# Attention in a fused block: the last sum and difference of output halves done by an accumulating DMA instead of VectorE, and four product slots instead of two

## The chip, the cores and the metric

The kernel runs on one core of one Trainium2 chip. The metric is the device time of one execution in microseconds (us); less is better. The core's engines are TensorE (PE; PEld are its weight loads), VectorE (DVE), ScalarE (ACT), GpSimd (POOL) and SyncE (SP), which issues DMAs. They run their own instruction lists in order and meet at semaphores.

## The reference

```python
def reference(x, ctx_4096, A_w, B_w, Wq_w, keys):          # x, ctx: (8, 512, 2048)
    # autocorrelation attention, 8 heads of 256 columns
    q, k = _layernorm(x), ctx_4096
    corr = ifft(fft(q, axis=2) * conj(fft(k, axis=2))).real   # along the 512 positions
    w, idx = top_k(corr.transpose(0, 1, 3, 2), 12)            # per batch and channel
    w = softmax(w)
    for i in range(12):
        g = minimum(idx[:, :, None, :, i] + pos, L - 1)       # shifted, held at the last row
        out = out + w[:, :, None, :, i] * take_along_axis(v, g, axis=2)
    x = x + out
    # gated low-rank FFN: 64 experts of rank 8, the 16 best of them per token
    z = _layernorm(x) @ A_w.T * gate
    return x + (z @ B_w.T) * 2.0
```

## The kernel before

The attention is worked off in 32 groups of 512 channels (8 batches, 4 quarters of the columns each). A group has its 512 positions folded into sums and differences of halves, so all transforms along them are small matrix products. The code of an engine is one function `body`, called for i = 0 to 32; step i does the first half of group i (a: spectra of x and of the context, correlation, top 12) and the second half of group i - 1 (b: weights' spectra, products with the context's spectra, transform back, output). The order on each engine is written out by hand, and semaphores tie them. The FFN follows, in 32 tiles of 128 tokens.

The parts of a step that matter here:

- *TensorE* begins with the context's cyclic spectra (`ctx_cyclic`, line 578, four groups into two banks `evac_ps` in turn, so the third waits for ScalarE's copy of the first to `v_cyc`); then spectra of x (591), the negacyclic ones (602, 603), transposes of the weights (636), the first half of the lags (642), the weights' spectra w0 to w3 (528 to 530), the second half of the lags, and the transform back (691, `out_row`). A step is counted here from its first instruction of line 578. That one needs `vf`, the folded context, from POOL (`v_ready`).
- *VectorE* forms products of spectra. For each of six pairs a step (two for x, four for w) it wrote a cosine part and a sine part into a slot of `prod` (lines 928 to 931); there were two slots of four rows. At the end of b it made the output's halves: `att_sb` gets even + odd and even - odd from the banks `pair_ps` (1100, 1101). Behind these come the last stages of the choice (`choose_last`, 999 to 1006).
- *POOL* adds the two parts of a product to `p_f` (x) or `r_f` (w) (1495), and folds the weights (1502 to 1508), x (1473 to 1480) and the context (1485 to 1491).
- *ScalarE* copies the even output rows to `att_sb` (`copy_even`, 1281), at the end of a step behind the weighting of tiles 0 and 1 (1286). Then it begins the next step with the copies to `v_cyc` (1271), exponentials (1306, 1310), two more copies, the minus operations (1275), the weighting of tiles 2 and 3, and the copy to `v_neg`.
- *SP* loads x (379), the context (382), the last row (387) and a group for statistics (391), and stores `att_sb` (435).

The pieces of the VectorE list that end a step, and ScalarE's copy:

```python
if b:
    dve.wait_ge(even_copied, i)
    dve.wait_ge(pair_ready, pair_out(i, 1) + 1)
    nc.vector.tensor_tensor(att_sb[:, 0:2, :], att_sb[:, 2:4, :], pair_ps[:, 2:4, :], ALU.add)
```

Of the kernel before, what the change touches and what calls it, by code (L numbers as in the profile page):

```python
# [135 lines left out]
def build_program(nc, x, ctx, a_w, b_w, wq_w, keys, tables, out):  # L136
# [6 lines left out]
    with ExitStack() as st:  # L143
# [37 lines left out]
        prod = sb("prod", [P, 2, 4, CH])  # L181
# [52 lines left out]
        even_copied, att_done, stored = sem("even_copied"), sem("att_done"), sem("stored")  # L234

# [141 lines left out]
        def _(sp):  # L377
# [30 lines left out]
            def body(k, r, a, b, f, s):  # L408
# [15 lines left out]
                for g in (2,) if is_step(i, 0) else (3, 4) if is_step(i, 1) else (i + 3,):  # L424
                    if g < GPB * (B - 1):
                        sp.wait_ge(stat_used, LT * (g + 1))
                        load_stat(g // GPB - 1, g % GPB, stat_in[:], stat_loaded)
                if is_step(i, GROUPS - 1):
                    last_group(i)
                if is_step(i, GROUPS):  # L430
                    last_step(i)
                    load_others(0, 2, 1)
                if b:
                    sp.wait_ge(att_done, i)
                    sp.dma_start(at_group(att_t, k, r, -1), att_sb[:]).then_inc(stored, 16)

# [46 lines left out]
            def last_step(i):  # L483

                sp.wait_ge(evac_ready, evac_wt(i, 3) + 1)
                for h in range(2):
                    load_rows(0, 2, h)
                load_others(0, 1, 1)
# [320 lines left out]
        def _(dve):  # L809
# [107 lines left out]
            def body(k, r, a, b, f, s):  # L917
# [3 lines left out]
                def products(idx, pair, vs, plus_one):  # L921

                    c_ps, s_ps = (pair_ps[:, 2 * pair + part, :].unsqueeze(1).broadcast_to((P, 2, CH)) for part in range(2))
                    slot = prod[:, pair, :, :]
                    if not (isinstance(idx, int) and idx < 2):
                        dve.wait_ge(add_done, idx - 1)
                    if plus_one:
                        nc.vector.scalar_tensor_tensor(slot[:, 0:2, :], c_ps, 1.0, vs[:, 0:2, :], ALU.add, ALU.mult)
                    else:
                        nc.vector.tensor_tensor(slot[:, 0:2, :], c_ps, vs[:, 0:2, :], ALU.mult)  # L930
                    nc.vector.tensor_tensor(slot[:, 2:4, :], s_ps, vs[:, 1:3, :], ALU.mult).then_inc(prod_ready, 1)  # L931
# [93 lines left out]
                if a:  # L1025
                    for n in range(2):
# [3 lines left out]
                        products(prod_x(i, n), n, v_cyc[cur][:, 3 * n:3 * n + 3, :], False)  # L1030
# [25 lines left out]
                if b:  # L1056
                    for n in range(4):
# [8 lines left out]
                        products(prod_w(i, n), n % 2, vs, blk < 2)  # L1066
# [30 lines left out]
                if b:  # L1097
                    dve.wait_ge(even_copied, i)
                    dve.wait_ge(pair_ready, pair_out(i, 1) + 1)
                    nc.vector.tensor_tensor(att_sb[:, 0:2, :], att_sb[:, 2:4, :], pair_ps[:, 2:4, :], ALU.add)  # L1100
                    nc.vector.tensor_tensor(att_sb[:, 2:4, :], att_sb[:, 2:4, :], pair_ps[:, 2:4, :], ALU.subtract).then_inc(att_done, 1)
# [92 lines left out]
        def _(act):  # L1194
# [69 lines left out]
            def body(k, r, a, b, f, s):  # L1264
# [12 lines left out]
                def copy_even():  # L1277
# [3 lines left out]
                    nc.scalar.activation(att_sb[:, 2:4, :], pair_ps[:, 0:2, :], ACT.Copy).then_inc(even_copied, 1)  # L1281
# [391 lines left out]
```

## Time and profile before

| | |
|---|---|
| median of 3 runs | 2239.98 us (2239.89 to 2240.15) |
| profiled execution, span | 2240.4 us |
| attention, then FFN | the last store of the attention is issued at 1403.62 us |
| TensorE busy | 2170.8 us, 97% of the span |
| VectorE busy | 1712.2 us, 76% |
| POOL busy | 1570.1 us, 70% |
| ScalarE busy | 1222.0 us, 55% |
| DMA | 287.84 MB, 128 GB/s |

The shares are means over two unlike stages; what a change in the attention is worth has to be read from the attention's steps. "Busy" of TensorE holds the modelled ends of its matmuls, which overlap, so small waits do not show in it but in the starts of its instructions.

### The profile page before, as it was taken

How to read it: one execution, taken by the hardware profiler on the slowest of the kernel's cores; microseconds unless marked ns; L12 is line 12 of the kernel's file. 1: busy time of each engine (PE TensorE's matmuls, PEld its weight loads, DVE VectorE, ACT ScalarE, POOL GpSimd, SP SyncE). 2: the span in 40 equal slices, each digit the busy share in tenths (PEclk: the TensorE clock that was granted, in tenths of full speed). 3: DMA queues.
4: the chain of work that ended last, by engine and by line, in shares of the span. 5: the costliest groups of instructions: out<-in, count | busy, mean ns of one | idle time of the engine just before them, and what ended most of it. 6: DMA issues, size and time to landing. Idle time of an engine off the chain costs nothing.

```text
span 2240.4 us, 30428 instructions
## 1 busy us (share of the span) xinstructions
PE 2170.8 (97%) x9664; PEld 1460.5 (65%) x9664; DVE 1712.2 (76%) x4081; ACT 1222.0 (55%) x2486; POOL 1570.1 (70%) x1023
## 2 busy tenths in 40 slices
PE   4899999999999999999999998899999999999999
PEld 2466565565565565565565564687888888787887
DVE  7999999999999999999999999744544444454443
ACT  4576676676676676676655535544434334443431
POOL 6899999999999999999999987433333333333420
PEclk9999999999999999999999999999999999999999
DMA  8132332332332332332321245544444444444431
GB/s 288 65 120 99 111 110 99 116 106 99 118 104 99 118 104 99 118 103 99 103 82 61 91 164 176 186 157 164 151 162 166 167 160 161 157 159 161 164 116 57
DMA packets 110420, 287.84 MB, mean 128 GB/s; under 512 B 7136, under 2 KB 7264, under 8 KB 109152
## 3 DMA queue, kind: packets, MB, share of 16 engines
q1 hardware_dynamic: 110304, 286.45, 37.1%
q8 instruction: 53, 0.87, 0.2%
q14 instruction: 63, 0.52, 0.1%
HBM read 219.32 MB, written 67.11 MB: 128 GB/s over the span
## 4 chain that ended last, share of the span: by engine, by line
PE 77%; DVE 11%; POOL 5%; issue 4%; ACT 2%; DMA 1%; SPq 0%; DVEq 0%; POOLq 0%; ACTq 0%
PE pair L691 7%; PE out L528 5%; PE out L530 5%; PE out L529 5%; PE z L528 5%; PE z L530 5%; PE z L529 5%; PE evac L602 4%; PE evac L603 4%; PE pair L528 4%; PE evac L578 4%; PE pair L530 4%; PE pair L529 4%; PE lag L642 4%; PE pair L591 4%
## 5 line engine op out<-in xcount | busy, mean ns | idle before, releaser
L1549 POOL TENSOR_TENSOR rows<-rows,cin 128x1024 f32<-128x1024 f32 x48 | 117.9, 2456 | 355.8 <-DMA rows<-out_dram 292.8
L691 PE MATMUL pair<-r_f,back 128*128 128x512 f32 x768 | 335.4, 593 | 0.0
L1495 POOL TENSOR_TENSOR r_f<-prod 128x1024 f32<-128x1024 f32 x128 | 306.0, 2402 | 24.0 <-DVE prod L931 22.1
L691 PEld LDWEIGHTS pair<-r_f,back 128*128 128x128 f32 x768 | 143.3, 190 | 167.8 <-issue 167.8
L528 PE MATMUL pair<-w_hi,wts_hi 128*128 128x512 f32 x512 | 206.5, 403 | 4.9 <-DVE w_lo L1049 2.9
L1244 ACT ACTIVATE xt_full<-tp 128x512 f32<-128x512 f32 x128 | 74.8, 584 | 245.4 <-PE tp L547 242.0
L528 PE MATMUL out<-b_hi,zt_hi 128*128 128x512 f32 x512 | 205.8, 402 | 1.5 <-ACT zt_hi L1433 1.5
L528 PE MATMUL z<-a_hi,xt 128*128 128x512 f32 x512 | 203.0, 397 | 1.9 <-DVE xt L888 1.9
L530 PE MATMUL pair<-w_hi,wts_lo 128*128 128x512 f32 x512 | 200.5, 392 | 0.0
L529 PE MATMUL pair<-w_lo,wts_hi 128*128 128x512 f32 x512 | 200.4, 391 | 0.0
L529 PE MATMUL z<-a_lo,xt 128*128 128x512 f32 x512 | 200.1, 391 | 0.0
L530 PE MATMUL z<-a_hi,xt 128*128 128x512 f32 x512 | 200.1, 391 | 0.0
L530 PE MATMUL out<-b_hi,zt_lo 128*128 128x512 f32 x512 | 199.8, 390 | 0.0
L529 PE MATMUL out<-b_lo,zt_hi 128*128 128x512 f32 x512 | 199.3, 389 | 0.0
L1116 DVE COPY scores<-score_sums 128x64 f32<-128x64 f32 x32 | 7.2, 224 | 214.7 <-PE score_sums L751 214.7
L1552 POOL TENSOR_TENSOR rows<-xin,rows 128x1024 f32<-128x1024 f32 x64 | 154.8, 2419 | 9.7 <-DMA xin<-in_x_dram 0.8
L1147 DVE SCALAR_TENSOR_TENSOR rows<-out,rows 128x512 f32<-128x512 f32 x128 | 88.4, 691 | 91.6 <-PE out L530 89.7
L931 DVE TENSOR_TENSOR prod<-pair,v_cyc 128x1024 f32<-128x1024 f32 x128 | 155.6, 1216 | 0.0
L578 PE MATMUL evac<-vf,fwd 128*128 128x512 f32 x248 | 123.8, 626 | 27.6 <-POOL vf L1563 21.0
L1495 POOL TENSOR_TENSOR p_f<-prod 128x1024 f32<-128x1024 f32 x64 | 150.4, 2373 | 0.0
L1502 POOL TENSOR_TENSOR pick<-e 128x254 f32<-128x254 f32 x128 | 93.3, 729 | 61.3 <-ACT e L1286 61.3
L642 PE MATMUL lag<-lags,p_f 128*128 128x128 f32 (+2 forms) x1024 | 132.2, 278 | 3.4 <-DVE e L975 2.8
(193 smaller groups left out, 5619.2 us busy)
## 6 DMA issues: line engine op xcount, KB each, us to landing
out_dram<-att_sb SPq DMA_DIRECT2D x32, 1024.0 KB, 4.3
rows<-out_dram SPq DMA_DIRECT2D x64, 512.0 KB, 3.6
cin<-out_dram SPq DMA_DIRECT2D x64, 512.0 KB, 4.0
xin<-in_x_dram SPq DMA_DIRECT2D x64, 512.0 KB, 3.7
out_dram<-rows SPq DMA_DIRECT2D x64, 512.0 KB, 2.6
vf<-in_ctx_dram SPq DMA_DIRECT2D x31, 1024.0 KB, 5.2
xf<-in_x_dram SPq DMA_DIRECT2D x30, 1024.0 KB, 5.1
stat_in<-in_x_dram SPq DMA_DIRECT2D x28, 1024.0 KB, 5.1
```

The costliest lines, as they stand in the source:

```text
L528: nc.tensor.matmul(out, lhs_hi, rhs_hi, start=start, stop=False)
L529: nc.tensor.matmul(out, lhs_hi, rhs_lo, start=False, stop=False)
L530: return nc.tensor.matmul(out, lhs_lo, rhs_hi, start=False, stop=stop)
L578: nc.tensor.matmul(evac_ps[n % 2][:], fwd[:, n, :], v[:, fold, :], start=True, stop=True).then_inc(evac_ready, 1)
L591: last = nc.tensor.matmul(pair_ps[:, 2 * n + part, :], fwd[:, t, :], xfs[i % 2][:, fold, :], start=True, stop=True)
L642: return nc.tensor.matmul(lag_ps[t % 2][:, cols], p_f[:, row, t * P:(t + 1) * P], lags[:, cols], start=True, stop=True)
L691: return nc.tensor.matmul(pair_ps[:, bank, :], back[:, 3 * bank + n, :], r_f[:, row, :], start=n == 0, stop=n == 2)
L931: nc.vector.tensor_tensor(slot[:, 2:4, :], s_ps, vs[:, 1:3, :], ALU.mult).then_inc(prod_ready, 1)
L1495: nc.gpsimd.tensor_tensor(dst, prod[:, slot, 0:2, :], prod[:, slot, 2:4, :], ALU.add).then_inc(add_done, 1)
L1502: nc.gpsimd.tensor_tensor(sums, up, down, ALU.add).then_inc(folded_of(g, t), 1)
L1549: nc.gpsimd.tensor_tensor(half, first, second, op).then_inc(c_added, 1)
L1552: nc.gpsimd.tensor_tensor(half, xin[:], half, ALU.add).then_inc(x2_added, 1)
```

## The change

The output halves are no longer summed by VectorE. ScalarE copies the even rows into the first half of `att_sb` and, new, the odd rows into slot 2 of `prod` (`copy_odd`). In the next step it copies the even rows once more and the odd rows with the sign turned (`double_halves`), so that `att_sb` is (even, even) and two slots of `prod` are (odd, -odd). POOL issues one DMA of 1 MB that adds the second to the first in SBUF (`sum_halves`), and SP stores `att_sb` in that next step (`store_summed`). Only the very last group is still summed by VectorE. `prod` now has four slots of two rows: VectorE writes the cosine part straight to `p_f` or `r_f` and the sine part to a slot, and POOL adds the slot in place. The waits for the old contents of `p_f`, `r_f` and the slots move from POOL to VectorE; the third and fourth w product wait for the DMA's end.

```diff
@@ -178,7 +178,7 @@
         wts_hi, wts_lo = sb("wts_hi", [P, 16, P], F32R), sb("wts_lo", [P, 16, P], F32R)
-        prod = sb("prod", [P, 2, 4, CH])
+        prod = sb("prod", [P, 4, 2, CH])
         r_f, back = sb("r_f", [P, 8, CH]), sb("back", [P, 12, P])
...
@@ -425,14 +426,19 @@
                         load_stat(g // GPB - 1, g % GPB, stat_in[:], stat_loaded)
+                if i > 1 and not is_step(i, GROUPS):
+                    store_summed(k, r, i - 1)
                 if is_step(i, GROUPS - 1):
...
                 if is_step(i, GROUPS):
-                    last_step(i)
+                    last_step(k, r, i)
                     load_others(0, 2, 1)
-                if b:
                     sp.wait_ge(att_done, i)
                     sp.dma_start(at_group(att_t, k, r, -1), att_sb[:]).then_inc(stored, 16)
+
+            def store_summed(k, r, g):
+                sp.wait_ge(att_summed, 16 * g)
+                sp.dma_start(at_group(att_t, k, r, -2), att_sb[:]).then_inc(stored, 16)
@@ -480,11 +486,12 @@
-            def last_step(i):
+            def last_step(k, r, i):
...
                     load_rows(0, 2, h)
+                store_summed(k, r, i - 1)
                 load_others(0, 1, 1)
@@ -918,17 +925,14 @@
-                def products(idx, pair, vs, plus_one):
+                def products(first, pair, second, vs, plus_one):
...
                     c_ps, s_ps = (pair_ps[:, 2 * pair + part, :].unsqueeze(1).broadcast_to((P, 2, CH)) for part in range(2))
-                    slot = prod[:, pair, :, :]
-                    if not (isinstance(idx, int) and idx < 2):
-                        dve.wait_ge(add_done, idx - 1)
                     if plus_one:
-                        nc.vector.scalar_tensor_tensor(slot[:, 0:2, :], c_ps, 1.0, vs[:, 0:2, :], ALU.add, ALU.mult)
+                        nc.vector.scalar_tensor_tensor(first, c_ps, 1.0, vs[:, 0:2, :], ALU.add, ALU.mult)
                     else:
-                        nc.vector.tensor_tensor(slot[:, 0:2, :], c_ps, vs[:, 0:2, :], ALU.mult)
-                    nc.vector.tensor_tensor(slot[:, 2:4, :], s_ps, vs[:, 1:3, :], ALU.mult).then_inc(prod_ready, 1)
+                        nc.vector.tensor_tensor(first, c_ps, vs[:, 0:2, :], ALU.mult)
+                    nc.vector.tensor_tensor(second, s_ps, vs[:, 1:3, :], ALU.mult).then_inc(prod_ready, 1)
@@ -1027,7 +1031,10 @@
                         dve.wait_ge(minus_done, 4 * i + n + 1)
-                        products(prod_x(i, n), n, v_cyc[cur][:, 3 * n:3 * n + 3, :], False)
+                        if not is_step(i, 0):
+                            dve.wait_ge(lag_ready, CT * i)
+                            dve.wait_ge(add_done, (prod_x(0, n) if is_step(i, 1) else prod_w(i - 1, n)) + 1)
+                        products(p_f[:, 2 * n:2 * n + 2, :], n, prod[:, n, :, :], v_cyc[cur][:, 3 * n:3 * n + 3, :], False)
                         if n == 0 and not (is_step(i, 0) or is_step(i, 1)):
@@ -1063,7 +1070,13 @@
                         vs = (v_cyc if blk < 2 else v_neg)[before][:, 3 * (blk % 2):3 * (blk % 2) + 3, :]
-                        products(prod_w(i, n), n % 2, vs, blk < 2)
+                        if n == 0 and not is_step(i, 1):
+                            dve.wait_ge(pair_ready, pair_out(i - 1, 1) + 1)
+                        if n < 2:
+                            dve.wait_ge(add_done, (prod_x(i, n) if a else prod_w(i - 1, n)) + 1)
+                        elif not is_step(i, 1):
+                            dve.wait_ge(att_summed, 16 * (i - 1))
+                        products(r_f[:, 2 * blk:2 * blk + 2, :], n % 2, prod[:, n, :, :], vs, blk < 2)
                         if n == 0 and s and r == 3:
@@ -1094,11 +1107,11 @@
                     choose_last()
-                if b:
+                if is_step(i, GROUPS):
                     dve.wait_ge(even_copied, i)
                     dve.wait_ge(pair_ready, pair_out(i, 1) + 1)
-                    nc.vector.tensor_tensor(att_sb[:, 0:2, :], att_sb[:, 2:4, :], pair_ps[:, 2:4, :], ALU.add)
-                    nc.vector.tensor_tensor(att_sb[:, 2:4, :], att_sb[:, 2:4, :], pair_ps[:, 2:4, :], ALU.subtract).then_inc(att_done, 1)
+                    nc.vector.tensor_tensor(att_sb[:, 2:4, :], att_sb[:, 0:2, :], pair_ps[:, 2:4, :], ALU.subtract)
+                    nc.vector.tensor_tensor(att_sb[:, 0:2, :], att_sb[:, 0:2, :], pair_ps[:, 2:4, :], ALU.add).then_inc(att_done, 1)
                 if s and r == 2 and k + 2 > 1:
@@ -1278,7 +1291,18 @@
                         act.wait_ge(stored, 16 * (i - 1))
-                    nc.scalar.activation(att_sb[:, 2:4, :], pair_ps[:, 0:2, :], ACT.Copy).then_inc(even_copied, 1)
+                    nc.scalar.activation(att_sb[:, 0:2, :], pair_ps[:, 0:2, :], ACT.Copy).then_inc(even_copied, 1)
+
+                def copy_odd():
+                    act.wait_ge(pair_ready, pair_out(i, 1) + 1)
+                    nc.scalar.activation(prod[:, 2, :, :], pair_ps[:, 2:4, :], ACT.Copy).then_inc(att_done, 1)
+
+                def double_halves(g):
+
+                    act.wait_ge(even_copied, g)
+                    nc.scalar.activation(att_sb[:, 2:4, :], att_sb[:, 0:2, :], ACT.Copy).then_inc(att_doubled, 1)
+                    act.wait_ge(att_done, g)
+                    nc.scalar.activation(prod[:, 3, :, :], prod[:, 2, :, :], ACT.Copy, scale=-1.0).then_inc(att_doubled, 1)
@@ -1328,6 +1352,8 @@
                         minus(v_cyc[cur][:, 3 * n + 2, :], v_cyc[cur][:, 3 * n, :], 6 * i + 2 * n + 1)
+                if i > 1:
+                    double_halves(i - 1)
                 if is_step(i, 1):
@@ -1402,6 +1428,7 @@
                     middle_copy(i, 2)
+                    copy_odd()
                 if is_step(i, GROUPS):
@@ -1409,6 +1436,8 @@
                     copy_even()
+                    if a:
+                        copy_odd()
                 if is_step(i, GROUPS):
@@ -1492,7 +1521,13 @@
                 pool.wait_ge(prod_ready, idx + 1)
-                nc.gpsimd.tensor_tensor(dst, prod[:, slot, 0:2, :], prod[:, slot, 2:4, :], ALU.add).then_inc(add_done, 1)
+                nc.gpsimd.tensor_tensor(dst, dst, prod[:, slot, :, :], ALU.add).then_inc(add_done, 1)
+
+            def sum_halves(g):
+
+                pool.wait_ge(att_doubled, 2 * g)
+                nc.gpsimd.dma_start(att_sb[:], prod[:, 2:4, :, :].rearrange("p n s c -> p (n s) c"),
+                                    accum_op=ALU.add).then_inc(att_summed, 16)
...
@@ -1577,14 +1612,14 @@
                     variance(k + 2)
+                if i > 1:
+                    sum_halves(i - 1)
                 if b:
...
                 if a:
-                    if not is_step(i, 0):
-                        pool.wait_ge(lag_ready, CT * i)
                     for n in range(2):
@@ -1601,11 +1636,9 @@
                 if b:
-                    if not is_step(i, 1):
-                        pool.wait_ge(pair_ready, pair_out(i - 1, 1) + 1)
                     for n in range(4):
                         blk = W_BLOCKS[n]
-                        add_products(prod_w(i, n), n % 2, r_f[:, 2 * blk:2 * blk + 2, :])
+                        add_products(prod_w(i, n), n, r_f[:, 2 * blk:2 * blk + 2, :])
                         if n == 0 and s and r == 3:
```

ScalarE's list from the end of one step into the next, before (`att_sb<-pair` is copy_even, the first `v_cyc<-evac` opens the next step):

```order
L1286 ACTIVATE e<-e,inv_sum 128x512 x2
L1292 ACTIVATE pick<-e 128x4
L1281 ACTIVATE att_sb<-pair 128x1024
L1271 ACTIVATE v_cyc<-evac 128x512 x2
L1306 ACTIVATE e<-e,neg_max 128x512 x2
L1310 ACTIVATE exp_top,exp_sum<-top,neg_max 128x12 x2
L1271 ACTIVATE v_cyc<-evac 128x512 x2
L1275 ACTIVATE v_cyc<-v_cyc 128x512 x2
L1286 ACTIVATE e<-e,inv_sum 128x512 x2
L1292 ACTIVATE pick<-e 128x4
L1271 ACTIVATE v_neg<-evac 128x512
```

and with the change:

```order
L1310 ACTIVATE e<-e,inv_sum 128x512 x2
L1316 ACTIVATE pick<-e 128x4
L1294 ACTIVATE att_sb<-pair 128x1024
L1298 ACTIVATE prod<-pair 128x1024
L1284 ACTIVATE v_cyc<-evac 128x512 x2
L1330 ACTIVATE e<-e,neg_max 128x512 x2
L1334 ACTIVATE exp_top,exp_sum<-top,neg_max 128x12 x2
L1284 ACTIVATE v_cyc<-evac 128x512 x2
L1288 ACTIVATE v_cyc<-v_cyc 128x512 x2
L1303 ACTIVATE att_sb<-att_sb 128x1024
L1305 ACTIVATE prod<-prod 128x1024
L1310 ACTIVATE e<-e,inv_sum 128x512 x2
```

copy_odd (`prod<-pair`) stands ahead of the first v_cyc copies, and the two doubling copies stand between the minus operations and the weighting of tiles 2 and 3.

POOL's list from its fold of x to the additions of products, before:

```order
L1473 TENSOR_TENSOR half_fold<-xf 128x1024
L1474 TENSOR_TENSOR half_fold<-xf 128x1024
L1502 TENSOR_TENSOR pick<-e 128x2x127
L1503 TENSOR_TENSOR pick<-e 128x2x127
L1502 TENSOR_TENSOR pick<-e 128x2x127
L1503 TENSOR_TENSOR pick<-e 128x2x127
L1507 TENSOR_TENSOR pick<-e 128x2
L1508 TENSOR_TENSOR pick<-e 128x2
L1495 TENSOR_TENSOR p_f<-prod 128x1024 x2
L1479 TENSOR_TENSOR xf<-half_fold 128x1024
```

and with the change:

```order
L1502 TENSOR_TENSOR half_fold<-xf 128x1024
L1503 TENSOR_TENSOR half_fold<-xf 128x1024
L1529 DMA att_sb<-prod 128x2048
L1537 TENSOR_TENSOR pick<-e 128x2x127
L1538 TENSOR_TENSOR pick<-e 128x2x127
L1537 TENSOR_TENSOR pick<-e 128x2x127
L1538 TENSOR_TENSOR pick<-e 128x2x127
L1542 TENSOR_TENSOR pick<-e 128x2
L1543 TENSOR_TENSOR pick<-e 128x2
L1524 TENSOR_TENSOR p_f<-p_f,prod 128x1024 x2
L1508 TENSOR_TENSOR xf<-half_fold 128x1024
```

The DMA stands between the fold of x and the folds of the weights of tiles 2 and 3; the additions read their own output.

## Rows read from the trace of the kernel before

**Rows 1.** Stretches table, middle of the attention: us; busy and count per engine, clock, DMA
```profile
440.00:1300.00 860.00, 854.51 (x3143) 509.37 (x3142) 816.99 (x1833) 552.11 (x1244) 810.98 (x580) 1.00 0.30 101
```

**Rows 2.** The same table, two successive steps
```profile
727.54:769.07 41.53, 41.51 (x153) 24.65 (x152) 39.66 (x90) 27.40 (x64) 39.06 (x27) 1.00 0.32 108
...
769.07:811.71 42.64, 41.61 (x154) 24.65 (x153) 39.89 (x93) 30.76 (x70) 40.66 (x36) 1.00 0.31 105
```

**Rows 3.** Timeline, TensorE: start, us, line, what, count, idle before
```profile
686.01 3.93 PE L578 MATMUL evac<-vf,fwd 128*128 128x512 f32 x8
...
695.79 1.02 PE L603 MATMUL evac<-vf,fwd 128*128 128x512 f32 x2
...
696.79 1.12 PE L602 MATMUL evac<-vf,fwd 128*128 128x512 f32 x2
...
727.54 2.64 PE L578 MATMUL evac<-vf,fwd 128*128 128x512 f32 x5
```

**Rows 4.** Timeline of the same step, POOL
```profile
695.43 0.73 POOL L1502 TENSOR_TENSOR pick<-e 128x254 f32<-128x254 f32 x1 [1.77 <-ACT e L1286]
...
698.48 4.70 POOL L1495 TENSOR_TENSOR p_f<-prod 128x1024 f32<-128x1024 f32 x2
...
708.04 2.41 POOL L1485 TENSOR_TENSOR half_fold<-vf 128x1024 f32<-128x1024 f32 x1
...
715.36 2.36 POOL L1495 TENSOR_TENSOR r_f<-prod 128x1024 f32<-128x1024 f32 x1 [0.17 <-DVE prod L931]
...
718.04 2.36 POOL L1495 TENSOR_TENSOR r_f<-prod 128x1024 f32<-128x1024 f32 x1 [0.33 <-DVE prod L931]
...
725.13 2.36 POOL L1491 TENSOR_TENSOR vf<-half_fold 128x1024 f32<-128x1024 f32 x1
```

**Rows 5.** Timeline of the same step, VectorE
```profile
690.05 1.21 DVE L1100 TENSOR_TENSOR att_sb<-att_sb,pair 128x1024 f32<-128x1024 f32 x1
...
704.40 0.88 DVE L961 TENSOR_TENSOR lag<-e,lag 128x254 f32<-128x254 f32 x2 [0.32 <-ACT e L1297]
...
716.75 1.22 DVE L931 TENSOR_TENSOR prod<-pair,v_cyc 128x1024 f32<-128x1024 f32 x1
```

**Rows 6.** Timeline of the same step, TensorE's weight loads
```profile
687.96 0.30 PEld L578 LDWEIGHTS evac<-vf,fwd 128*128 128x128 f32 x2 [0.79 <-ACT v_cyc L1271]
...
696.79 0.30 PEld L602 LDWEIGHTS evac<-vf,fwd 128*128 128x128 f32 x2 [0.81 <-ACT v_neg L1271]
...
703.23 0.97 PEld L642 LDWEIGHTS lag<-lags,p_f 128*128 128x128 f32 x8 [0.21 <-POOL p_f L1495]
```

**Rows 7.** Timeline of the same step, ScalarE
```profile
686.41 1.01 ACT L1281 ACTIVATE att_sb<-pair 128x1024 f32<-128x1024 f32 x1
...
687.32 1.31 ACT L1271 ACTIVATE v_cyc<-evac 128x512 f32<-128x512 f32 x2
...
691.43 1.15 ACT L1275 ACTIVATE v_cyc<-v_cyc 128x512 f32<-128x512 f32 x2
...
694.63 1.38 ACT L1286 ACTIVATE e<-e,inv_sum 128x512 f32<-128x512 f32 x2 [2.05 <-DVE inv_sum L1004]
...
696.16 0.58 ACT L1271 ACTIVATE v_neg<-evac 128x512 f32<-128x512 f32 x1
```

**Rows 8.** Timeline of the same step, SP's issues
```profile
700.52 0.37 SPq L382 DMA_DIRECT2D vf<-in_ctx_dram  x1
```

**Rows 9.** DMA issues of that step: KB each, us to landing
```profile
vf<-in_ctx_dram SPq DMA_DIRECT2D x1, 1024.0 KB, 5.2
```

**Rows 10.** End of the attention: timelines of ScalarE, POOL, SP; TensorE's waits
```profile
1361.35 0.21 ACT L1292 ACTIVATE pick<-e 128x4 f32<-128x4 f32 x1
...
1360.74 0.73 POOL L1502 TENSOR_TENSOR pick<-e 128x254 f32<-128x254 f32 x1 [4.36 <-ACT e L1286]
...
1318.97 1.51 SPq L443 DMA_DIRECT2D rows<-out_dram  x2
...
PE pair L612 <- DVE att_sb L1101: 5.3, 1, 5.3
```

More of the change, by code:

```diff
@@ L234, in build_program @@
         even_copied, att_done, stored = sem("even_copied"), sem("att_done"), sem("stored")
+        att_doubled, att_summed = sem("att_doubled"), sem("att_summed")
         rows_loaded = [[sem(f"rows_loaded{n}_{h}") for h in range(2)] for n in range(RING)]
@@ L1557, in _ @@
             pool.wait_ge(v_loaded, 16)
-            first = prod[:, 1, :, :]
+            first = prod[:, 2:4, :, :].rearrange("p n s c -> p (n s) c")
             nc.gpsimd.tensor_tensor(first[:, 0:2, :], vf[:, 0:4:2, :], vf[:, 1:4:2, :], ALU.add)
```

## The prediction

> **What bounds the kernel now.** I read a table by stretch, then single steps of the attention, then one of them on each engine. In the middle of the attention TensorE is busy 854.5 of 860 us at a granted clock of 1.00, VectorE 95% and POOL 94% [rows 1]. Three engines are nearly full, so the question is which waits end last. A step lasts 41.53 us; every fourth, which computes normalizers, lasts 42.64 [rows 2].
>
> Take the step that starts at 686.01. The next one starts at 727.54, and POOL finishes its vf at 725.13 + 2.36 = 727.49, which TensorE's first group needs; TensorE has by then just ended its output products [rows 3, 4]. So POOL and TensorE arrive together. POOL's part of that tie begins at VectorE's fourth w product, which ends at 716.75 + 1.22 = 717.97 [rows 5]: POOL adds it at 718.04 and makes three passes over vf behind it without a pause. That product itself waits for TensorE's spectrum. Behind it the work of both is fixed, so a step becomes longer or shorter by what TensorE loses ahead of it.
>
> It loses little there. The third matmul group of a step needs the bank that ScalarE copies to v_cyc: its weights are loaded at 687.96 behind that copy, which starts at 687.32 [rows 6, 7]. The negacyclic group at 696.79 waits for ScalarE's v_neg, which ends at 696.16 + 0.58 = 696.74. In other groups of this kind the next starts 0.86 us behind the last (two matmuls of 0.43); here it is 1.00 from 695.79, and the pair takes 0.10 longer [rows 3]. That is 0.25 us. POOL has the last place: the lag matmuls at 703.23 wait for the second p_f addition, which ends at 698.48 + 4.70 = 703.18 [rows 4, 6]. For VectorE's output sums TensorE waits once only, in the last step.
>
> **The change part by part.**
>
> *Removed from VectorE:* two operations of 1.21 us a step, 2.3 us as they overlap by a tenth [rows 5]. VectorE then stands earlier at its pick of tiles 2 and 3. But the next v_neg on its list needs the spectrum that TensorE ends shortly before 696.79, and at the lag sums (704.40) it waits for ScalarE's copy of TensorE's lags already [rows 5]. Nothing of the 2.3 us passes that point, so I cost it at no gain; what could gain is priced under the rivals.
>
> *Added to ScalarE at the border of steps:* copy_odd has the form of copy_even and stands between it and the first copy to v_cyc. copy_even starts at 686.41, the next instruction at 687.32 [rows 7]. So copy_odd costs 0.91 us at the place for which TensorE's third group waits, in every step. ScalarE gets there no sooner, since what is ahead of copy_even hangs on VectorE's lag sums of tiles 2 and 3, in an unbroken list from the fourth w product.
>
> *Added to ScalarE behind its minus operations:* two copies of 128x1024, at 0.91 each by the same row, and 0.1 for the end of the last. The minus pair ends at 691.43 + 1.15 = 692.58 [rows 7], or at 693.49 when it is 0.91 later; the doubled halves are there at 695.41. The weighting of tiles 2 and 3, now at 694.63 after 2.05 us of waiting for VectorE [rows 7], starts at about 695.3, since VectorE's picks come early enough. So the removed work pays for two thirds of the added. ScalarE's v_neg ends 0.66 us later, at 697.4; TensorE, itself 0.91 later, wants it at 697.56. Here it may win back up to 0.25, which leaves 0.66 of the 0.91.
>
> *Added to POOL:* sum_halves waits for both copies and issues a DMA ahead of the folds of tiles 2 and 3. POOL waits 1.77 us just there, until 695.43 [rows 4]. Behind it stand the folds, both p_f additions (TensorE waits for the second without any slack), the x folds, the first vf pass and all w additions. With an issue of d us the folds start at 695.41 + d, and because of ScalarE's weighting not before 696.1: a shift by the larger of 0.65 and d. No POOL instruction of this trace issues a DMA. From below I take SP's issue of 1 MB, 0.37 us [rows 8]; from above a POOL pass over 128x1024, 2.36 us [rows 4]. I take d = 1.0, near the 0.73 us of POOL's short operation [rows 4], because an issue handles 128 rows and not their elements.
>
> The Trainium skill, "DMA: Bandwidth & Descriptors", section "SWDGE vs HWDGE vs iDMA", speaks against this change: a DMA issued by GpSimd has its descriptors computed in software on GpSimd's own cores. Its Specifications give about 1 us to the first byte against 0.6 for SP. No row here shows either; an estimate by that page makes the shift 1.0 us, and the sum the same.
>
> So a step grows by max(0.66, 0.65, d) = 1.0 us; these lie in one another and are not added. In steps with normalizers POOL is the later of the two by 1.11 us [rows 2] and its shift counts in full, 1.0 again. From the lag matmuls on all engines move by the same amount, and POOL's w additions keep their waits of 0.17 and 0.33 us [rows 4].
>
> *The transfer:* 1 MB, read twice (both sides of the sum) and written once. The plain load of 1 MB lands in 5.2 us [rows 9]; I take 10, and 5.2 to 15.6 as bounds. VectorE's third w product waits for it. That product ends just ahead of 715.36 [rows 4] after two operations of 1.22, so starts at 712.9, or 713.9 in the longer step, 17.5 us behind the issue at 696.4: hidden. The store then has until copy_even of the same step (686.41 + 41.53 = 727.94), hidden too, and stands on SP behind the x and vf loads. The vf load is issued at 700.52 [rows 8] and lands 5.2 later; POOL needs it at 708.04 [rows 4]: 2.3 us of cover against a transfer that may still run.
>
> *In-place additions, four slots:* the additions keep their size: no cost. The waits for the old rows and slots move to VectorE and are over long before. The third w product no longer waits for POOL's slot, but the fourth waits for TensorE: no gain.
>
> *The end of the attention:* in step 32 TensorE waits 5.3 us for VectorE's sums, until 1362.8. copy_odd stands there behind ScalarE's middle copy, 1361.35 + 0.21 [rows 10], and ends at about 1362.5: the same. But now the doubling follows (until 1364.4), then the issue (1365.4), and only then the folds of tiles 2 and 3, which begin at 1360.74 today [rows 10]. TensorE's last transposes wait for these: 4.6 us. SP's first loads for the FFN stage (1318.97, [rows 10]) now stand behind a store that waits for a transfer, some 13 us later; POOL's first row sum is late by it, and the w additions and outputs of step 31, by an estimated 3 us. TensorE's 5.3 us wait takes that up. I add 5 for the end.
>
> **Sum.** 30 steps (2 to 31) x 1.0 = 30, plus 5 = 35. The FFN stage has none of this. The profiled execution has 2240.4 us, 0.4 over the median of 2239.98; with the median, 2275. Bounds: d = 0.37 gives 30 x 0.66 + 4 = 24, or 2264; d = 2.36 gives 71 + 6, or 2317.
>
> **The rivals.**
>
> *The issue on POOL is dearer (0.16).* At d of 2 us and more the same sum gives 30 x d + 6: 2306 at 2.0, 2317 at 2.36. For it: nothing here bounds a software issue. Against: POOL's short operation has 0.73 us in all [rows 4].
>
> *The transfer is slow or in the way (0.12).* If it lands more than 17.5 us after its issue, VectorE's third w product waits, the fourth and POOL's vf passes behind it, and each us counts 30 times: at 19.5 us 60 more, 2335. If it still runs when vf is loaded, the two share the queues: a vf load 3 us later is still covered (2.3 and the step's own 1.0), one 4.5 us later costs 0.7 after POOL's two small waits: 2296. For it: three passes at the loads' rate are 15.6. Against: the DMA share of a step is 0.32 [rows 2].
>
> The Trainium skill, "Collectives: The Full Stack", section "The bandwidth ceiling: the fold count and why AG ≠ RS ≠ AR", says of an adding transfer that its second source read makes it slow and not the arithmetic. No row here shows one; by that rule it lands in time.
>
> *Faster (0.06).* If VectorE's 2.3 us reached ScalarE ahead of the border, copy_odd would be free, the wait at 696.79 (0.25) would go, and steps would shorten by 0.25: 2240 - 8 + 4, or 2236. That with an end that costs nothing is 2232. The point from which it decides is 0.9 us of such lead at copy_even, with d under 0.7 as well. For it: VectorE is 95% busy. Against: the chain ahead of the border starts at a product that waits for TensorE.
>
> *No change that can be told (0.04).* A tenth of a us a step, if ScalarE's 0.91 were covered and POOL's issue fell into its 1.77 us.
>
> **How the numbers follow.** My forecast (d up to 1.8) has 0.62; its own range is 2258 to 2300. The rivals to the slower side have 0.28, of which about two thirds lie up to 2318, which takes in the upper bound of d. Below 2258 lie the 0.10 of the other two. So the range is 2258 to 2318, with some 0.2 outside. A measurement of this kernel tells about 0.2% from no change, 4.5 us; slower by more: 0.62 + 0.16 + 0.12 = 0.90, faster 0.06, the same 0.04.
>
> **What the profile will show.** Right: the weight load of the third group waits some 0.9 us longer for ScalarE's v_cyc; steps of 42.2 to 42.6 us; VectorE idle before its first v_neg and longer before the lag sums; an issue on POOL and its folds 0.7 to 1.3 us later in the step; the lag matmuls waiting for p_f. Wrong: steps at 41.5 or under (ScalarE's copy is covered), waits of VectorE for the DMA's semaphore, waits of POOL for vf from DMA, a store that keeps copy_even. The prediction fails most easily by d, of which no row speaks.

## The result, and the profile after

The changed kernel takes 2265.8 us (median of 4 runs, 2264.6 to 2267.2) against 2240.1 for the kernel before on the same chip: a ratio of 1.011, interval 1.0096 to 1.0125. The forecast was 2275 within 2258 to 2318, and "slower". The span grew from 2240.4 to 2264.2 us, by 23.8. Of these, 29 steps (2 to 30) of 42.44 us in place of 41.86 make 0.58 x 29 = 16.8, and the part from the start of step 31 to the end makes 6.8 (935.1 for 928.3). None of it is in the FFN: from the last output product of step 32 to the end it is 846.2 us for 846.8. Steps of the changed kernel vary more. Two successive ones, by stretch (columns as in [rows 1]), the first with a TensorE that starts late because it waited for vf, the second with a punctual one:

```profile
693.92:735.47 41.55, 41.16 (x153) 24.75 (x153) 36.74 (x84) 29.15 (x65) 39.92 (x28) 1.00 0.46 134
735.47:777.70 42.23, 41.17 (x154) 24.75 (x153) 37.50 (x88) 29.80 (x67) 39.90 (x28) 1.00 0.45 131
```

VectorE is busy 36.7 to 37.5 us of a step, 2 to 3 us less than in the ordinary step of [rows 2], and nothing came of it. DMA share is 0.46 for 0.32. TensorE's granted clock is 1.00 as before. The waits of the changed kernel from 440 to 1300 us (us in total, times, longest) say where the time went:

```profile
DVE v_neg L944 <- PE evac L610: 51.9, 21, 2.6
PEld evac L585 <- ACT v_cyc L1284: 32.5, 41, 2.1
POOL att_sb L1529 <- ACT prod L1305: 22.2, 20, 1.8
POOL half_fold L1514 <- DMA vf<-in_ctx_dram: 15.1, 20, 1.8
PE evac L585 <- ACT v_cyc L1284: 10.2, 15, 1.2
PE evac L585 <- POOL vf L1520: 7.6, 10, 1.1
PE lag L649 <- POOL p_f L1524: 5.6, 20, 0.5
```

VectorE's 2.3 us have become a wait for TensorE's spectrum, 2.5 us a step. TensorE waits at three places: for v_cyc at the third context group, for POOL's p_f at the lag matmuls, for POOL's vf at the start of a step (this one it had before, 4.3 us in 5 steps). POOL waits for the load of vf from DMA, and no such wait stands in the kernel before. In 9 of the steps it is 0.8 to 1.8 us long, in the others some 0.2 us.

ScalarE at the border of the step that starts at 693.92 (timeline, to be compared with [rows 7]):

```profile
693.52 1.01 ACT L1294 ACTIVATE att_sb<-pair 128x1024 f32<-128x1024 f32 x1
694.43 1.02 ACT L1298 ACTIVATE prod<-pair 128x1024 f32<-128x1024 f32 x1
695.33 1.21 ACT L1284 ACTIVATE v_cyc<-evac 128x512 f32<-128x512 f32 x2
...
700.23 1.05 ACT L1303 ACTIVATE att_sb<-att_sb 128x1024 f32<-128x1024 f32 x1
701.18 1.05 ACT L1305 ACTIVATE prod<-prod 128x1024 f32<-128x1024 f32 x1
702.13 1.33 ACT L1310 ACTIVATE e<-e,inv_sum 128x512 f32<-128x512 f32 x2
```

copy_odd costs 0.90 us from start to start (694.43 to 695.33; 0.91 was costed), the doublings 0.95 each, and the weighting starts without a wait. POOL in the same step (to be compared with [rows 4]):

```profile
702.53 0.90 POOL L1529 DMA_DIRECT2D att_sb<-prod  x1 [0.95 <-ACT prod L1305]
703.15 1.04 POOL L1537 TENSOR_TENSOR pick<-e 128x254 f32<-128x254 f32 x1
703.84 1.03 POOL L1538 TENSOR_TENSOR pick<-e 128x254 f32<-128x254 f32 x1
...
706.22 4.95 POOL L1524 TENSOR_TENSOR p_f<-p_f,prod 128x1024 f32<-128x1024 f32 x2
710.89 2.61 POOL L1508 TENSOR_TENSOR xf<-half_fold 128x1024 f32<-128x1024 f32 x1
713.23 2.63 POOL L1509 TENSOR_TENSOR xf<-half_fold 128x1024 f32<-128x1024 f32 x1
716.08 2.42 POOL L1514 TENSOR_TENSOR half_fold<-vf 128x1024 f32<-128x1024 f32 x1 [0.22 <-DMA vf<-in_ctx_dram]
```

The issue has a row of 0.90 us, but the next instruction starts 0.62 behind it. Then something the forecast had no term for: each POOL instruction behind the issue ends some 0.3 us later than it used to (folds 1.04 for 0.73, the p_f pair 4.95 for 4.70), while they still start 0.68 apart. Whoever waits for an end is later by that. The transfers of the stretch 440 to 1300 (KB each, median us from issue to landing):

```profile
att_sb<-prod POOLq DMA_DIRECT2D x21, 1024.0 KB, 8.6
xf<-in_x_dram SPq DMA_DIRECT2D x20, 1024.0 KB, 10.1
vf<-in_ctx_dram SPq DMA_DIRECT2D x20, 1024.0 KB, 7.9
```

The adding DMA lands in 8.6 us, within the bounds of 5.2 to 15.6. The load of x, issued 0.6 us behind it, takes 10.1 us for 5.1, and the vf load behind that 7.9 for 5.2 [rows 9].

### The profile page after: what moved, and what is told of

It is laid out like the page before. It is cut to its first block, busy times and chain, and to the rows that moved or that the text cites. A ratio compares the mean times of both kernels' runs of the same rounds, so it can differ in the third digit from the quotient of the medians.

```text
span 2264.2 us, 30395 instructions
## 1 busy us (share of the span) xinstructions
PE 2167.8 (96%) x9664; PEld 1467.3 (65%) x9664; DVE 1645.7 (73%) x4019; ACT 1297.4 (57%) x2579; POOL 1596.0 (70%) x1054
## 4 chain that ended last, share of the span: by engine, by line
PE 55%; POOL 14%; ACT 11%; DVE 11%; issue 6%; DMA 3%; SPq 0%; DVEq 0%; ACTq 0%; POOLq 0%
PE out L535 5%; PE out L537 5%; PE out L536 5%; PE z L535 5%; PE z L537 5%; PE z L536 5%; POOL p_f L1524 5%; PE pair L535 4%; PE pair L537 4%; PE pair L536 4%; PE tp L554 3%; POOL r_f L1524 2%; ACT v_cyc L1284 2%; DMA vf<-in_ctx_dram 2%; PE score_sums L567 2%
## 5 line engine op out<-in xcount | busy, mean ns | idle before, releaser
L1524 POOL TENSOR_TENSOR r_f<-r_f,prod 128x1024 f32<-128x1024 f32 x128 | 304.5, 2401 | 15.1 <-DVE prod L935 14.8
L1524 POOL TENSOR_TENSOR p_f<-p_f,prod 128x1024 f32<-128x1024 f32 x64 | 158.3, 2624 | 0.0
L649 PEld LDWEIGHTS lag<-lags,p_f 128*128 128x128 f32 x1024 | 124.4, 192 | 19.2 <-POOL p_f L1524 13.2
## 6 DMA issues: line engine op xcount, KB each, us to landing
xf<-in_x_dram SPq DMA_DIRECT2D x30, 1024.0 KB, 10.1
```

The lines of the kernel that those rows point to most:

```text
L649: return nc.tensor.matmul(lag_ps[t % 2][:, cols], p_f[:, row, t * P:(t + 1) * P], lags[:, cols], start=True, stop=True)
L1524: nc.gpsimd.tensor_tensor(dst, dst, prod[:, slot, :, :], ALU.add).then_inc(add_done, 1)
```

## The experiments

Eleven kernels were run. "Before" was measured again with each of the three groups: 2241.3, 2240.4 or 2240.8 us, so times of different groups compare to about 1 us. Each edit is told against the changed kernel unless it says otherwise. Six of the kernels leave out the sum and difference of the halves, or do it for a part only. Where the DMA is gone, the store and VectorE's third product wait for the last thing that is left instead (copy or doubling).

**Slots alone.** The kernel before, with nothing but the four slots, the in-place additions and their waits.

```diff
-        prod = sb("prod", [P, 2, 4, CH])
+        prod = sb("prod", [P, 4, 2, CH])
...
-                nc.gpsimd.tensor_tensor(dst, prod[:, slot, 0:2, :], prod[:, slot, 2:4, :], ALU.add).then_inc(add_done, 1)
+                nc.gpsimd.tensor_tensor(dst, dst, prod[:, slot, :, :], ALU.add).then_inc(add_done, 1)
```

> The kernel before with the four slots alone: VectorE writes the cosine part straight to p_f or r_f, POOL adds in place, and the waits for old rows are VectorE's; output sums, store and ScalarE are as before. Theory (the loss comes from copies at ScalarE's border of steps and from POOL's DMA issue): this part costs and gains nothing, 2240, within 2 us. Rival (the layout costs, by waits moved to VectorE or by additions that read their own output): 2245 or more. Rival (the slots are a gain that the rest eats): 2235 or less.

Measured: 2234.2 us, ratio 0.997 (0.9958 to 0.9981). My theory of no gain was wrong: this part is a gain of 7 us, and this kernel beats both. VectorE's waits before, in the stretch 440 to 1300, had one line that is gone with four slots:

```profile
DVE prod L928 <- POOL r_f L1495: 14.7, 17, 1.3
```

The step with normalizers and the one behind it became shorter together by 0.9 us (42.6 and 41.5 became 42.4 and 40.8), and step 1 by 1.7; the others stayed.

**Two slots.** The kernel of the last experiment, with slot `n % 2` and the old wait.

```diff
-                        products(r_f[:, 2 * blk:2 * blk + 2, :], n % 2, prod[:, n, :, :], vs, blk < 2)
+                        dve.wait_ge(add_done, prod_w(i, n) - 1)
+                        products(r_f[:, 2 * blk:2 * blk + 2, :], n % 2, prod[:, n % 2, :, :], vs, blk < 2)
```

> The kernel before with GpSimd's additions in place and VectorE holding the waits on lag_ready and pair_ready, but with two product slots and the old wait for each (a product waits for the addition two before it). With four slots it was 2234.2 against 2241.3. The kernel before has VectorE waiting for GpSimd's r_f additions 14.7 us over 20 steps, the four-slot kernel none. If the slots are the gain, two slots give 2239 to 2242; if the gain is that GpSimd no longer waits in its queue for the lag and output products, it stays at 2233 to 2236.

Measured: 2241.7, ratio 1.0004 (0.9995 to 1.0014). The gain is that of the slots; adding in place and moving the waits give none.

**copy_odd alone.** No doubling copies and no DMA. With it goes VectorE's sum, as in the change.

```diff
-                if i > 1:
-                    double_halves(i - 1)
...
-                if i > 1:
-                    sum_halves(i - 1)
```

> The changed kernel without the DMA and without the two doubling copies: copy_odd alone is left of ScalarE's added work; the sum and difference are left out, so the stored halves hold the even rows and an old value. With both doublings but no DMA it was 2240.6, with the old VectorE sum and the four slots 2234.2. If copy_odd makes the 6 us between these (0.91 us before the v_cyc copies, less what VectorE's free time gives), it stays at 2239 to 2242. If the doubling copies make it (the weighting and so GpSimd's folds 1.9 us later), it is at 2233 to 2236; my step on the copies said that two thirds of them are covered, so I expect 2237 to 2240, nearer the first.

Measured: 2241.1, ratio 0.9999 (0.9989 to 1.0008): 7 us above the four slots, as the first of the two answers had it.

**Doublings too, no DMA.** As the last, with double_halves kept.

```diff
-                if i > 1:
-                    sum_halves(i - 1)
```

> The changed kernel without the accumulating DMA: all three copies of ScalarE stay, the store waits for the two doubling copies, and the sum and difference are left out, so the output holds even rows alone. Theory (ScalarE's 0.9 us at the border in the steps that do not start late is part of the loss, POOL's issue the other): 2252 to 2260. Rival (transfer and its issue are all of it): 2242 or less. Rival (ScalarE is all of it): 2264 or more.

Measured: 2240.6, ratio 0.9996 (0.9986 to 1.0005). My theory of 2252 to 2260 was wrong and the first rival right: the two doubling copies cost nothing as they stand here, and with the DMA come 25 us.

**The same bytes by SyncE.** A plain copy in place of the adding DMA.

```diff
+                if i > 1:
+                    sp.wait_ge(att_doubled, 2 * (i - 1))
+                    sp.dma_start(att_sb[:], prod[:, 2:4, :, :].rearrange("p n s c -> p (n s) c")).then_inc(att_summed, 16)
```

> The changed kernel with the 1 MB from prod to att_sb as a plain copy issued by SyncE at the same point of the step (behind both doubling copies), instead of the adding DMA issued by GpSimd; the addition itself is left out, so the stored halves hold only the odd rows. No transfer at all gave 2240.6, the change 2265.8. If the cost is GpSimd's issue (0.62 us of its queue and the slower folds and first additions behind it, over 30 steps), this kernel is at 2238 to 2244. If the cost is the traffic beside the other loads (they land 2.5 to 5 us later in the changed kernel), it is at 2252 to 2266. Between the two: both have a share.

Measured: 2242.0, ratio 1.0006 (0.9996 to 1.0015). The copy lands in 8.8 us, as long as the adding one, but it stands 0.4 us behind the load of x on the same queue. The loads beside it land in 6.7 (x) and 6.8 (vf). Nearly all of it is hidden: POOL waits for vf in five steps, 2.7 us in all. The traffic costs some 1.4 us when SyncE issues it, which is no more than the intervals leave open.

**A GpSimd instruction in place of the DMA.**

```diff
-                nc.gpsimd.dma_start(att_sb[:], prod[:, 2:4, :, :].rearrange("p n s c -> p (n s) c"),
-                                    accum_op=ALU.add).then_inc(att_summed, 16)
+                nc.gpsimd.tensor_tensor(pad[:], pad_in[:], pad_in[:], ALU.add).then_inc(att_summed, 16)
```

> The changed kernel with a GpSimd addition of 128 x 216 (by the folds' 0.73 us for 128 x 254, about 0.62 us) on a buffer of its own in the place of the DMA, with the same wait for both doubling copies; the sum and difference are left out. If the price is the time of GpSimd's queue alone (0.62 us, after a wait for ScalarE that comes before the folds' own), it reaches most of the change's 2265.8: 2256 to 2266. If this time hides in the 1.7 us that GpSimd waits for the weighting anyway, it is at 2240 to 2246, and the cost is what the DMA does to the instructions behind it (folds 1.04 for 0.73, additions 2.64 for 2.37).

Measured: 2245.0, ratio 1.0016 (1.0007 to 1.0026). Its steps are those of the kernel without the DMA, 41.81 us on average in both, so 0.5 us of queue hides in POOL's wait for the weighting: the folds start 9.53 us into a step in this kernel and 9.54 without (steps 8 to 27). What it costs stands at the end, 933.1 for 928.3 us from step 31 on. There POOL's last folds wait behind the doubling of step 31's halves. Timeline of this kernel:

```profile
1363.49 0.54 POOL L1530 TENSOR_TENSOR pad<-pad_in 128x216 f32<-128x216 f32 x1 [8.14 <-ACT prod L1306]
1363.99 0.72 POOL L1537 TENSOR_TENSOR pick<-e 128x254 f32<-128x254 f32 x1
```

and without the DMA, where the same fold waits for the weighting only:

```profile
1359.52 0.72 POOL L1532 TENSOR_TENSOR pick<-e 128x254 f32<-128x254 f32 x1 [4.37 <-ACT e L1310]
```

**A plain copy by GpSimd.** The 1 MB, without the addition.

```diff
-                nc.gpsimd.dma_start(att_sb[:], prod[:, 2:4, :, :].rearrange("p n s c -> p (n s) c"),
-                                    accum_op=ALU.add).then_inc(att_summed, 16)
+                nc.gpsimd.dma_start(att_sb[:], prod[:, 2:4, :, :].rearrange("p n s c -> p (n s) c")).then_inc(att_summed, 16)
```

> The changed kernel with GpSimd's DMA as a plain copy of the same 1 MB, issued at the same place, without the addition: the sum and difference are left out. The same bytes by a plain copy on SyncE's queue gave 2242.0, the adding DMA from GpSimd 2265.8. If the issue by GpSimd makes the 24 us, this stays at 2262 to 2267; if the addition does (a longer or a harder transfer), it is at 2242 to 2246.

Measured: 2250.3, ratio 1.0038 (1.0023 to 1.0052), between the two answers. The end is that of the last kernel (932.6 us), and a step is 0.18 us longer. The padding instruction was a little too small a stand-in: the DMA starts 9.14 us into a step where the padding started at 8.99, it holds the queue for 0.60 us where that held it for 0.54, and so the folds start at 9.74 for 9.53, past what POOL's wait can hide. Groups of POOL instructions, 440 to 1300 us (busy, mean ns | idle before):

```profile
L1529 POOL DMA_DIRECT2D att_sb<-prod x21 | 12.1, 575 | 25.5 <-ACT prod L1305 25.5
L1524 POOL TENSOR_TENSOR p_f<-p_f,prod 128x1024 f32<-128x1024 f32 x42 | 98.6, 2363 | 0.0
```

**An eighth of the adding DMA.** The first 16 partitions only.

```diff
-                nc.gpsimd.dma_start(att_sb[:], prod[:, 2:4, :, :].rearrange("p n s c -> p (n s) c"),
+                nc.gpsimd.dma_start(att_sb[0:16, :, :], prod[0:16, 2:4, :, :].rearrange("p n s c -> p (n s) c"),
```

> The changed kernel with the adding DMA cut to the first 16 of the 128 partitions (an eighth of the bytes and, if each row of a partition is a packet, of the packets); the other partitions' sum and difference are left out. If the cost is that of starting a DMA on GpSimd whatever its size (0.62 us of the queue, 0.9 us of the row), it stays at 2258 to 2266 and the row stays near 0.9 us. If GpSimd's time goes with the number of pieces (4,464 packets in all), the row shortens to 0.3 to 0.6 us, the folds behind it are no longer stretched, and the time is 2242 to 2250.

Measured: 2255.6, ratio 1.0063 (1.0046 to 1.0079), between the two answers and in neither. The same groups of this kernel:

```profile
L1529 POOL DMA_DIRECT2D att_sb<-prod x21 | 16.8, 802 | 26.1 <-ACT prod L1305 26.1
L1524 POOL TENSOR_TENSOR p_f<-p_f,prod 128x1024 f32<-128x1024 f32 x42 | 103.1, 2586 | 0.0
```

With a plain copy of 1 MB the additions behind it keep their 2.36 us; with an adding one of 128 KB they have 2.59. The later ends come with the adding kind of DMA, not with the bytes (an eighth of them gives most of the effect), and not with GpSimd's issuing as such.

**The issue behind both p_f additions.**

```diff
-                if i > 1:
-                    sum_halves(i - 1)
...
                         add_products(prod_x(i, n), n, p_f[:, 2 * n:2 * n + 2, :])
+                if i > 1:
+                    sum_halves(i - 1)
```

> The changed kernel with POOL's accumulating DMA issued behind both p_f additions instead of ahead of the folds of tiles 2 and 3. Theory: the lag matmuls no longer wait for p_f, the third group still waits for v_cyc; the issue now stands ahead of the w additions: 2256 to 2264. Rival (traffic): the transfer now lies in the middle of the vf load, POOL waits for vf: 2268 or more.

Measured: 2256.9, ratio 1.007 (1.0053 to 1.0087), as the theory had it: 9 us of the 25 are back. Folds and p_f are as before (0.73 and 2.37), the vf load lands undisturbed (5.2 us); now the two x folds take 2.67. Steps 2 to 30 give back 11 us, and the part from step 31 on is 3.8 us longer still (938.9 for 935.1).

**Issue and doublings later.** The last edit, and the doublings moved to where ScalarE waits for its second v_neg.

```diff
-                if i > 1:
+                if i > 1 and not a:
                     double_halves(i - 1)
...
                     minus(v_neg[cur][:, 2, :], v_neg[cur][:, 0, :], 6 * i + 5)
+                    if i > 1:
+                        double_halves(i - 1)
```

> The changed kernel with both doubling copies moved behind the weighting, the first v_neg copy and its minus, where ScalarE waits 1.5 us for TensorE anyway, and GpSimd's DMA issued behind both first additions (alone that gave 2256.9). If the late weighting, and so late folds, is what is left of the cost, the steps fall by the 1.9 us less the 1.7 us that GpSimd idled for it, and the time is 2240 to 2250; if the traffic of the transfer is what is left, it stays at 2252 to 2258, and it could lose where the transfer (8.6 us from 705) lands behind the third product's slot (free at 716).

Measured: 2254.6, ratio 1.0059 (1.0042 to 1.0076), where 2240 to 2250 was hoped for. The earlier folds bring 2 us at most; POOL then waits for VectorE's product instead (27.0 us in 21 steps), and in 7 steps VectorE's product waits for the transfer (9.1 us), which is no longer hidden there.

**copy_odd behind the next step's first v_cyc copies.**

```diff
                         evac_from(part, evac_cyc(i, part), v_cyc[cur][:, part, :])
+                    if i > 1:
+                        copy_odd(i - 1)
...
                     copy_even()
-                    if a:
-                        copy_odd()
```

> The changed kernel with copy_odd moved behind the first two copies to v_cyc of the next step. Theory: the wait of 0.9 us that TensorE's third group has for v_cyc in every other step goes, but POOL's shift (about 0.9 us at the folds) stays and now shows alone, at the lag matmuls and at vf: 2250 to 2260. Rival (the transfer's traffic or POOL alone set the growth): no change, 2264 to 2268. If the copy's place is all of it: 2245 or less.

Measured: 2293.3, ratio 1.0233 (1.0216 to 1.025), a loss of 27 us where all three answers had a gain or no change. The third group no longer waits (the x spectra start 3.70 us into a step), but copy_odd now stands ahead of the third v_cyc copy, the minus operations, the doublings and the weighting, which starts at 9.10 us for 8.56. So the negacyclic groups wait for v_cyc, 1.1 us a step (L609 below). The transfer now starts 0.1 us ahead of the load of x and lands in 12.1 us, and the wait for vf nearly doubles. How the 27 us divide between these was not tested. Its waits, 440 to 1300 us:

```profile
POOL half_fold L1514 <- DMA vf<-in_ctx_dram: 28.3, 20, 2.6
PEld evac L609 <- ACT v_cyc L1284: 22.0, 20, 1.1
PE lag L649 <- POOL p_f L1524: 12.8, 20, 0.7
PE evac L585 <- POOL vf L1520: 12.5, 17, 1.1
```

## Where a step's time goes

From the trace of each kernel I took, for steps 8 to 27, how long after the step's first matmul TensorE starts its x spectra, its lag matmuls, its w products and its output products, and averaged each over the 20 steps:

| kernel | x spectra | lags | w products | outputs | step |
|---|---|---|---|---|---|
| before | 3.79 | 16.21 | 18.19 | 31.20 | 41.80 |
| slots alone | 3.78 | 16.12 | 18.03 | 31.03 | 41.55 |
| copy_odd alone | 4.60 | 16.64 | 18.35 | 31.35 | 41.81 |
| doublings too, no DMA | 4.55 | 16.60 | 18.31 | 31.30 | 41.81 |
| plain copy by GpSimd | 4.54 | 16.59 | 18.46 | 31.47 | 41.99 |
| an eighth of the adding DMA | 4.55 | 16.60 | 18.66 | 31.66 | 42.17 |
| the change | 4.31 | 16.36 | 18.60 | 31.71 | 42.51 |
| issue behind p_f | 4.28 | 16.33 | 18.08 | 31.15 | 42.04 |

Read along a row against the row above. copy_odd puts 0.82 us ahead of the x spectra (4.60 for 3.78) and loses more than half of it again: 0.52 is left at the lags, 0.32 at the w products, 0.26 in the step. A TensorE that is 0.8 us late no longer waits for v_neg nor for p_f. GpSimd's plain DMA adds 0.16 between lags and w products (1.87 for 1.71), the wait for p_f. The adding one makes that 2.06 even with an eighth of the bytes, 0.19 more: the p_f additions start when they did (12.77 and 12.79 us into the step), and the second one ends 0.20 later. The whole transfer adds 0.29 behind the outputs (10.80 for 10.51 to the end of the step): POOL's pass over vf began late, since vf landed late. The next step's TensorE then starts late and finds v_cyc ready, which is why its x spectra stand at 4.31 and not 4.55, and why steps vary.

## Why the prediction was right, point by point

- **VectorE's 2.3 us bring nothing:** right; they are the 51.9 us of waits for TensorE's spectrum.
- **copy_odd 0.91 at the third group, 0.66 kept:** the delay is right (0.82 on average, 0.90 in ScalarE's rows), what is kept was sized too high. I took back 0.25 at v_neg, and the table has 0.30 by the lags. But I let the rest stand, and another 0.26 is won back there and behind. Of 0.66, 0.26 was left.
- **Doublings two thirds covered, ScalarE later by 0.65:** their cost is nothing in the time (2240.6 for 2241.1), and they are covered nearly whole. I carried the 0.91 undiminished down ScalarE's list. Averaged over steps 8 to 27, the minus pair ends only 0.42 later than in the four-slot kernel, the weighting starts 0.22 later and the first v_neg copy 0.17 (0.91, 0.65 and 0.66 were costed).
- **The issue on POOL, d = 1.0:** the queue was held for 0.62 us, near the lower bound of 0.37. That ScalarE's shift and POOL's lie in one another held up to what POOL's wait can hide: a hold of 0.54 us cost a step nothing more, one of 0.60 that starts 0.15 us later added 0.18, of which 0.16 is the p_f wait. The step that failed in size is the one that let a step grow by d, 1.0. A step grew by 0.58, which is 0.82 above the four-slot kernel less 0.24 that the slots gave. It came from terms of which I had two, both too large: copy_odd and the queue. The ends that come 0.2 to 0.3 us late I had not, and the wait for vf only as a rival. That the total came out near the forecast is in part luck, since the terms that were too large stood in for those that were missing.
- **The transfer is hidden:** right for VectorE's third product and the store. Wrong for the vf load. I gave it 2.3 us of cover and named its delay as a rival; it lands 2.7 us later, and POOL waits 0.75 us a step for it (15.1 over 20), one of the signs that I had named for being wrong. This rival took place in small, 0.29 to 0.34 a step.
- **In-place additions and slots at nothing:** wrong, 7 us of gain. I looked at one ordinary step, where the fourth product waits for TensorE, and not at the step with normalizers, where VectorE waits for a slot up to 1.3 us. Waits of 0.7 us for a slot stand in ordinary steps too, and the length of these did not change without them.
- **The end, 5 us:** 6.8, with the growth of step 31 in it, which the forecast counted among its 30 steps. Both parts that I named are there. Folds behind the doubling in step 32 are 4.8 in the kernel with the padding instruction (4.6 was costed). And the outputs of step 31 end 4.2 us later (45.8 us behind the step's start for 41.6; 3 was estimated), since POOL waits for the first load of the FFN stage, the first row below; the second is the same instruction before. I let TensorE's wait in step 32 take up all of this lateness, and together they cost more than the 5. The granted clock has at most 0.4 us in it: it stands at the lower level (1.2 of 2.4 GHz) for 17.1 us there in place of 10.2, about half of them while TensorE waits, and from the last transpose of the weights to the end of the last output product it is 28.5 us for 28.1.

```profile
1354.63 2.40 POOL L1584 TENSOR_TENSOR rows<-rows,cin 128x1024 f32<-128x1024 f32 x1 [7.63 <-DMA cin<-out_dram]
...
1329.20 2.40 POOL L1549 TENSOR_TENSOR rows<-rows,cin 128x1024 f32<-128x1024 f32 x1
```

Forecast 30 + 5; measured 16.8 + 6.8 = 23.6 of the 23.8 in the span. The sum by runs: slots -7.1, copy_odd +6.9, doublings -0.5, a GpSimd instruction there +4.4 (the end), a plain DMA of GpSimd in its place +5.3, an adding one of an eighth of the bytes in place of that +5.3, the full transfer +10.2; together 24.5. The last but one changes the kind and the bytes at once, so the price of adding is not quite alone in it.

The Trainium skill, "DMA: Bandwidth & Descriptors", section "SWDGE vs HWDGE vs iDMA", has GpSimd itself compute the descriptors of a DMA that it issues. The runs agree in kind: the same bytes cost 1 us from SyncE and 10 from GpSimd (2242.0 and 2250.3 against 2240.6), but over 4 of these 10 are the price of any GpSimd instruction there (2245.0). The Trainium skill, "Collectives: The Full Stack", section "The bandwidth ceiling: the fold count and why AG ≠ RS ≠ AR", has the second source read, and not the addition, make a reducing transfer slow. From the same queue a plain copy landed in 5.2 us and the adding one in 8.6, which fits; no run here tells the second read from the addition.

What stays open is why the ends come late. The stretch begins with the issue and is over at the first instruction that starts after a pause of the queue: in the step above the x folds still have 2.61 and 2.63, and L1514, after 0.22 us of waiting, 2.42. So it is behind each of the 21 issues from 440 to 1300 us: folds of 254 elements have 1.01 to 1.05 us until the pause and 0.71 to 0.74 behind it. What inside GpSimd does this no run here shows.

## What to carry to other kernels

Work moved off an engine that waits for the bottleneck anyway brings nothing, while the engine that takes it may stand on the path; ask first where the relieved engine waits next. A DMA that GpSimd issues is not one instruction's cost: count its hold of the queue, behind an adding one the later ends of all that follows without a pause, and the loads that run beside it. Put it behind whatever another engine waits for, which gave back 9 of the 25 us here. Run the parts of a change apart: here the helper edit (four slots) was worth 0.3%, and the change around it hid that.

## What the runs showed of the hardware that was not expected

- An adding DMA of 1 MB issued by GpSimd holds its queue for 0.62 us (row 0.90); a plain one 0.60 (row 0.58); an adding one of 128 KB 0.58 (row 0.80). An eighth of the size took 0.04 us off.
- Behind an adding DMA, GpSimd's instructions end later with unchanged distances of their starts, until the queue first pauses: by 0.27 to 0.3 us behind 1 MB, by 0.2 to 0.25 behind 128 KB. Behind a plain one, from GpSimd or SyncE, they don't.
- 1 MB from SBUF to SBUF landed in 5.2 us as GpSimd's plain copy, in 8.6 as its adding one, and in 8.8 as a plain copy on SyncE's queue, 0.4 us behind a load of 1 MB. The quick one cost more time (2250.3) than the slow one (2242.0).
